# A selective state-space layer on one Trainium2 core: C rows by DMA broadcast, four of sixteen C products on GpSimd, three states in the ring

## What is computed

```
xn = layernorm(x);  x_inner, z = split(xn @ W_in.T)          # 256 features each
u = silu(depthwise conv of x_inner, 4 taps, causal)
dt_low, B, C = split(u @ W_x.T, [64, 80])                    # B and C: 16 numbers a token
dt = clip(softplus(dt_low @ W_dt.T + b_dt) + 0.001, 0.001, 0.1)
per token:  h = exp(dt * A) * h + (dt * u) * B               # h: 256 features x 16 states
            y = sum over the 16 states of h * C
y = (y + u * D_param) * silu(z);   x = x + y @ W_out.T
```

## Time and profile before

| | us |
|---|---|
| median of 3 runs | 4296.08 |
| the profiled execution | 4291.76 |
| its span | 4289.7 |
| VectorE busy in the span | 2998.2 (70%) |
| TensorE busy | 3517.0 (82%) |
| GpSimd busy | 1574.8 (37%) |
| ScalarE busy | 1881.7 (44%) |

### The profile page before, as it was taken

The page is one execution under the profiler, slowest core; times in us unless marked ns, Lnnn a source line. Parts: engine busy times, 40 slices in busy tenths (PEclk is TensorE's granted clock), DMA queues, the critical chain, the costliest instruction groups (busy, mean ns, idle before and its releaser), DMA issues. The chain is left out here.

```text
span 4289.7 us, 60121 instructions
## 1 busy us (share of the span) xinstructions
PE 3517.0 (82%) x21245; PEld 2138.2 (50%) x21300; DVE 2998.2 (70%) x6467; ACT 1881.7 (44%) x3383; POOL 1574.8 (37%) x1050
## 2 busy tenths in 40 slices
PE   5899999878999972777558888888859999999757
PEld 3666665556777762444323333333326666666423
DVE  7888887556777746333259999999975666666695
ACT  2555555325666630222146666666632223222224
POOL 2211110442111100688747877787741000011132
PEclk9999999989999975899879999999989999999868
DMA  6333332004444440233322222222220000000001
GB/s 145 85 80 79 79 79 59 1 13 108 98 98 98 99 131 9 40 44 43 71 69 67 79 69 66 64 79 68 66 71 1 1 1 1 1 1 1 10 0 40
DMA packets 196474, 237.43 MB, mean 55 GB/s; under 512 B 37554, under 2 KB 148883, under 8 KB 185924
## 3 DMA queue, kind: packets, MB, share of 16 engines
q1 hardware_dynamic: 170516, 214.93, 19.0%
q0 software_dynamic: 22528, 17.32, 2.9%
q10 hardware_dynamic: 3136, 1.35, 0.1%
HBM read 176.83 MB, written 55.51 MB: 54 GB/s over the span
## 5 line engine op out<-in xcount | busy, mean ns | idle before, releaser
L568 DVE TENSOR_REDUCE a_Mx<-a_Sx 128x2 f32<-128x512 f32 (+1 forms) x1024 | 590.8, 617 | 232.4 <-PE a_Sx L620 135.3
L2141 POOL TENSOR_TENSOR a_inp<-a_dtu,a_Bs 128x1024 f32<-128x1024 f32 x256 | 604.7, 2383 | 94.7 <-DVE a_h L2305 93.4
L2305 DVE TENSOR_TENSOR_SCAN a_h<-a_dA,a_inp 128x1024 f32<-128x1024 f32 x256 | 584.3, 2282 | 5.3 <-ACT a_dA L2233 5.3
L2395 PE MATMUL a_Y<-a_hc,g_ident 128*128 128x512 f32 x1024 | 520.0, 633 | 8.1 <-DVE a_hc L2315 8.0
L413 ACT ACTIVATE a_Pr<-a_Se 128x512 f32<-128x512 f32 x512 | 305.1, 596 | 410.9 <-DVE a_Se L562 219.4
L344 POOL TENSOR_TENSOR a_rest<-a_qk,a_parts 128x512 f32<-128x512 f32 x64 | 75.2, 1175 | 987.5 <-ACT a_parts L396 987.5
L2233 ACT ACTIVATE a_dA<-a_dtA,a_A 128x512 f32<-128x512 f32 x512 | 331.4, 682 | 171.8 <-DVE a_h L2305 171.1
L1957 ACT ACTIVATE f_sg<-f_GB 128x512 f32<-128x512 f32 x272 | 162.4, 597 | 513.5 <-PE f_GB L2007 513.4
L617 PE MATMUL a_Sx<-att_Kp,att_Qp 96*128 96x256 bf16 (+1 forms) x2048 | 347.4, 262 | 48.9 <-DMA att_Qp<-a_crows 26.0
L1902 DVE TENSOR_TENSOR f_sg<-f_sg,f_UB 128x512 f32<-128x512 f32 x256 | 176.2, 688 | 283.1 <-PE f_CB L2014 256.1
L2040 PEld LDWEIGHTS f_OUT<-f_wd,f_hm 128*128 128x128 f32 x2176 | 286.2, 192 | 91.0 <-issue 81.9
(11 more groups left out here) (446 smaller groups left out, 7136.2 us busy)
## 6 DMA issues: line engine op xcount, KB each, us to landing
a_Bs<-a_brows SPq DMA_DIRECT2D x256, 256.0 KB, 3.2
att_Qp<-a_packing SPq DMA_DIRECT2D x192, 192.0 KB
att_Kp<-a_packing SPq DMA_DIRECT2D x192, 192.0 KB
a_packing<-a_parts SPq DMA_DIRECT2D x64, 384.0 KB
a_packing<-a_parts SPq DMA_DIRECT2D x64, 128.0 KB
g_x<-x SPq DMA_DIRECT2D x8, 512.0 KB, 7.3
f_sum<-g_x SPq DMA_DIRECT2D x1, 4096.0 KB, 13.2
f_w<-L_w SPq DMA_DIRECT2D x2, 2048.0 KB
```

The lines of the kernel that those rows point to most:

```text
L568: nc.vector.tensor_reduce(Mx[(k + 2 - (j < LATE)) % 2][:, t, 2 * jj:2 * jj + 2], Sx[t][:, 0:2 * wd].rearrange("p (h q) -> p h q", h=2), AX ...
L2141: nc.gpsimd.tensor_tensor(inp[n % Q][:], dtu[k][:], Bs[n % Q][:].unsqueeze(1).to_broadcast([P, CH, GT]), ALU.mult).then_inc(s["mulB"], 1)
L2305: nc.vector.tensor_tensor_scan(h[n % 2][:].rearrange("p c q -> p (c q)"), dA[m % 2][:].rearrange("p c q -> p (c q)"), inp[n % Q][:].rearra ...
L2395: nc.tensor.matmul(Y[c][:], ident[:], hc[n % Q][:, c], start=(n == 0), stop=(n == N - 1))\
```

## The change

- C rows now come like B rows: `brows` holds 32 rows, and SP issues a second DMA for each state, into `Cs[n % 4]` in SBUF. `spread_C`, `split`, the matrix `sel` and its load go away, as does the bf16 copy on ScalarE (L2204).
- The C product reads h and Cs. For n = 1, 4, 7 and 10 (`MOVED`) GpSimd does it, after its `mulB` of n + 3; for the other twelve VectorE does it.
- `h` has three buffers; the scan of m waits for the product of m - 3.
- The skip term is a float32 matmul with a diagonal matrix, two a group, that opens Y's sum. VectorE's step at n = 0 becomes yy = Y * sz (two products of 512), and GpSimd's product with sz goes away.
- The add to x and its statistics (n = 15) move behind VectorE's C product of n = 15.

```diff
-        h = [sc.sb(f"h{i}", [P, CH, GT]) for i in range(2)]
+        h = [sc.sb(f"h{i}", [P, CH, GT]) for i in range(HR)]
+        Q, HR = 4, 3
+        MOVED = (1, 4, 7, 10)
+        Cs = [sc.sb(f"Cs{i}", [P, GT]) for i in range(Q)]
+        diag = sc.sb("diag", [P, CH, P])
-        CC = sc.ps("CC", [P, GT])
-                 (bdt, "bdt"), (dpar, "dpar"), (lnw, "lnw"), (lnb, "lnb"), (la, "la"), (sel, "sel")]
+                 (bdt, "bdt"), (dpar, "dpar"), (lnw, "lnw"), (lnb, "lnb"), (la, "la")]
@@ block.sync @@
+                    if on(0):
+                        wait_product(sp, g * N + n - Q)
+                        sp.dma_start(Cs[n % Q][:], bass.AP(brows.tensor, (k * 2 * N + N + n) * GT, [[0, P], [1, GT]]))\
+                            .then_inc(c_in[n % Q], 16)
@@ block.gpsimd @@
+            def mulC(m, n):
+                wait(pool, c_in[n % Q], 16 * (m // Q + 1))
+                wait(pool, s["scanned"], m + 1)
+                wait(pool, s["y_mm"], CH * (m + 1 - Q))
+                C = Cs[n % Q][:].unsqueeze(1).to_broadcast([P, CH, GT])
+                nc.gpsimd.tensor_tensor(hc[n % Q][:], h[m % HR][:], C, ALU.mult).then_inc(s["mulC_pool"], 1)
-                    if on(-1) and n == 1:
-                        wait(pool, s["y_read"], g * CH)
-                        wait(pool, s["sz_ready"], g)
-                        wait(pool, s["out_mm"], g - 1)
-                        nc.gpsimd.tensor_tensor(yy[:], yy[:], sz[(k + 1) % 2][:], ALU.mult).then_inc(s["y_ready"], 1)
-                    if on(1) and n == 9:
-                        split(g + 1, (k + 1) % 2)
+                    if n - 1 in MOVED and on(0):
+                        mulC(g * N + n - 1, n - 1)
@@ block.vector @@
-                        nc.vector.scalar_tensor_tensor(out=yy[:, c], in0=u[k][:, c], scalar=dpar[:, c:c + 1],
-                                                       in1=Y[c][:], op0=ALU.mult, op1=ALU.add).then_inc(s["y_read"], 1)
+                        nc.vector.tensor_tensor(yy[:, c], Y[c][:], sz[k][:, c], ALU.mult).then_inc(s["y_read"], 1)
-                        wait(v, s["mulC"], m - 1)
+                        wait_product(v, m - HR)
-                    if on(0):
-                        wait(v, s["cc_mm"], m + 1)
+                    if on(0) and n not in MOVED:
+                        wait(v, c_in[n % Q], 16 * (m // Q + 1))
                         wait(v, s["scanned"], m + 1)
                         wait(v, s["y_mm"], CH * (m + 1 - Q))
-                        nc.vector.tensor_tensor(hc[n % Q][:], h[n % 2][:], CC[:].unsqueeze(1).to_broadcast([P, CH, GT]),
+                        nc.vector.tensor_tensor(hc[n % Q][:], h[m % HR][:], Cs[n % Q][:].unsqueeze(1).to_broadcast([P, CH, GT]),
                                                 ALU.mult).then_inc(s["mulC"], 1)
@@ block.tensor @@
-                    if on(0) and n < N - 1:
-                        spread_C(g * N + (n + 1), n + 1, k)
                             wait(pe, s["y_read"], CH * g)
+                            for c in range(CH):
+                                nc.tensor.matmul(Y[c][:], diag[:, c], u[k][:, c], start=True, stop=False)
-                        wait(pe, s["mulC"], g * N + n + 1)
+                        wait_product(pe, g * N + n)
```

More of the change, by code:

```diff
@@ L2098, in state_space, with by_vector, by_pool, wait_product @@
         loads = [(win, "win"), (cw, "cw"), (wdl, "wdl"), (wbc, "wbc"), (wdt, "wdt"), (wout, "wout"), (cbias, "cbias"),
-                 (bdt, "bdt"), (dpar, "dpar"), (lnw, "lnw"), (lnb, "lnb"), (la, "la"), (sel, "sel")]
+                 (bdt, "bdt"), (dpar, "dpar"), (lnw, "lnw"), (lnb, "lnb"), (la, "la")]
         U = 9
         b_in = [sc.sem(f"b_in{i}") for i in range(Q)]
+        c_in = [sc.sem(f"c_in{i}") for i in range(Q)]
+        def by_vector(m):
+            return m // N * (N - len(MOVED)) + sum(n not in MOVED for n in range(m % N + 1))
+        def by_pool(m):
+            return m // N * len(MOVED) + sum(n in MOVED for n in range(m % N + 1))
+        def wait_product(eng, m):
+            if m >= 0 and m % N in MOVED:
+                wait(eng, s["mulC_pool"], by_pool(m))
+            elif m >= 0:
+                wait(eng, s["mulC"], by_vector(m))
         @block.sync
@@ L2124, in _ @@
         def _(pool):
[L2125 to L2135, removed]
             def mulB(m, n, k):
@@ L2366, in front @@
                         .then_inc(s["f_mm"], 1)
-            def spread_C(m, n, k):
-                wait(pe, s["mulC"], m)
-                nc.tensor.matmul(CC[:], sel[:, N + n], bc[k][:], start=True, stop=True).then_inc(s["cc_mm"], 1)
             def step(g, k, on):
                 for n in range(N):
-                    if on(0) and n < N - 1:
-                        spread_C(g * N + (n + 1), n + 1, k)
-                    if on(1) and n == N - 1:
-                        wait(pe, s["bc_ready"], 2 * g + 4)
-                        spread_C(g * N + N, 0, (k + 1) % 2)
                     if on(1):
@@ L2392, in step @@
                             wait(pe, s["y_read"], CH * g)
-                        wait(pe, s["mulC"], g * N + n + 1)
+                            for c in range(CH):
+                                nc.tensor.matmul(Y[c][:], diag[:, c], u[k][:, c], start=True, stop=False)
+                        wait_product(pe, g * N + n)
                         for c in range(CH):
-                            nc.tensor.matmul(Y[c][:], ident[:], hc[n % Q][:, c], start=(n == 0), stop=(n == N - 1))\
+                            nc.tensor.matmul(Y[c][:], ident[:], hc[n % Q][:, c], start=False, stop=(n == N - 1))\
                                 .then_inc(s["y_mm"], 1)
             straight(pe, step, GROUPS, 1, back=1)
[L2401 to L2405, removed]
 def program(nc, a, out):
@@ L2457, in l2_attn @@
     w = {n: a["L2_" + n] for n in "win cw wdl wbc wdt wout cbias bdt dpar lnw lnb la".split()}
-    state_space(nc, res, "a4", {**w, "sel": a["c_bsel"]})
+    state_space(nc, res, "a4", w)
 def l2_ffn(nc, res, a):
@@ L2537, in layout @@
     o["L2f_bias"] = np.broadcast_to(i["L2_ffn_e_score_bias"].reshape(1, 1, 32), (P, G, 32))
-    for n, c in {**attention_constants(), **choose_constants(), **routed_constants(), **state_constants()}.items():
+    for n, c in {**attention_constants(), **choose_constants(), **routed_constants()}.items():
         o["c_" + n] = c
```

32 lines of the change are left out of this document (15 added, 17 removed).

## The result

The changed kernel takes 4461.12 us (median of 4 runs, 4460.09 to 4463.38), 1.0384 times the time before (95% interval 1.0371 to 1.0397), or +165.5 us against 4295.59, the median of the four runs of the kernel before that were timed with it. The forecast was 4384, range 4315 to 4450. The direction and the main mechanism were right; a second stall, of 88 us, was missed, and the time lies above the range.

What follows compares the result with a forecast made beforehand. VectorE was taken to set the pace. 16 x 2.6 for the states plus 15 x 3.45 at group edges minus 6 gives +87 us on 4291.8, and with 4.3 for the median 4384 us; range 4315 to 4450.

Steps and rivals of the forecast that it cites:

- The exclusion: VectorE products with two SBUF inputs and GpSimd products take turns at a lock held for a whole instruction; 79%.
- three states: In states 1 to 10, each cycle of three takes 11.4 us instead of 10.5; +2.6 us a group.
- the stretch from scan 10 to the next scan 1: The group's edge, 28.8 us before the change; claimed to grow by 2.4 to 4.5 us a group.
- The near tie: After scan 15, GpSimd and VectorE reach the lock 0.1 us apart; unsettled, so the middle, 3.45 us a group, was taken.
- the forecast's upper case: GpSimd goes first after scan 15: scan 1' ends at 33.3 us, +4.5 us a group.
- SP asks for C row n once product n-4 is done ... hidden: SP's extra C loads come over 10 us ahead of use; cost nothing, at worst 51 us.
- The sign that the forecast gave for being wrong: A Cs load named as releaser of VectorE; listed among signs that would show the forecast wrong.
- The range: 4315, a little under the lock-never-idle floor, to 4450, the roof plus a late C row each group (51 us).
- the 6 us off for start and tail: No `sel` load at the start, no GpSimd product in the tail, no first split and copy: 6 us off.
- moved add now covers that: At the group's edge, the moved add covers VectorE's yy being held up by Y at the lower clock.
- Rival 1: No exclusion in this layer: groups of 54.4 us, -6.0 a group, 4194 us; 9%.
- Rival 2: GpSimd wins the lock after scans and TensorE falls to 1.2 GHz: +6.6 us a group, 4490 us; 9%.
- Rival 3: Half an exclusion: instructions shut each other out for part of their time; 4289 us, no change; 3%.

Runs made afterwards that it cites:

- e3: The changed kernel with SP's store behind the loads of n = 11 and VectorE's twelve C products reading ones in PSUM (C left out there): 4220.86 us, ratio 0.9853.
- e1: The changed kernel with SP's store of the next B and C rows, and its wait, moved behind the loads of n = 11: 4375.4 us, ratio 1.0209.
- e7: The kernel before with only the skip term on TensorE, yy * sz on VectorE and the moved add; C as it was: 4277.17 us, ratio 0.9987.
- e4: e1 with MOVED empty, so VectorE does all sixteen C products from SBUF: 4346.51 us, ratio 1.0148.
- e8: e6 with GpSimd's split moved from n = 9 to n = 12: 4247.52 us, ratio 0.9885.
- e5: e1 with ScalarE copying each C row that VectorE needs from SBUF to a PSUM tile: 4302.21 us, ratio 1.0041.
- e6: e1 with VectorE's twelve states getting C in PSUM by the earlier split and spread matmuls, GpSimd's four rows by DMA: 4353.13 us, ratio 1.0162.

## Why the prediction was right and wrong

- **The exclusion** was right: that it would hold here, argued from the first layer's rows, is shown by e3. Its working held: three states 11.36 us for 11.4, products at 1.28 and 3.31 for 1.3 and 3.2 (its own timeline gives 3.3 for the second, from 5.88 to 9.19), the stretch from scan 10 to the next scan 1 33.16 us in e1 (2706.06 to 2739.22):

```profile
2706.06 4.46 DVE L2314 TENSOR_TENSOR_SCAN a_h<-a_dA,a_inp 128x1024 f32<-128x1024 f32 x2
...
2728.09 3.30 DVE L2324 TENSOR_TENSOR a_hc<-a_h,a_Cs 128x1024 f32<-128x1024 f32 x1
...
2736.30 3.00 DVE L2324 TENSOR_TENSOR a_hc<-a_h,a_Cs 128x1024 f32<-128x1024 f32 x1
2739.22 4.46 DVE L2314 TENSOR_TENSOR_SCAN a_h<-a_dA,a_inp 128x1024 f32<-128x1024 f32 x2
```

- **The near tie** at scan 15 goes to GpSimd in every group but the last, both in the changed kernel and in e1 (the product of n = 15 takes 3.3 us): 33.2 us, the forecast's upper case of 33.3, and not the middle. 15 x 0.9 = 14 us too little.
- **"SP asks for C row n once product n-4 is done ... hidden"** is the step that failed. The wait named there was the right one for the load itself, but the load is in a queue, and ahead of it, in the same step of the program, stood another wait: for the next group's bf. I counted the loads that came to SP's queue and not what they were put behind. The term stood at nothing in the sum and was bounded at 51 us, by the 3.2 us of one landing a group; it is 6.0 us a group, since the issue itself came late: 88.1 us of idle, 75 of them net. The sign that the forecast gave for being wrong, a Cs load named as what VectorE waits for, is what came. The trace of the kernel before could have shown it. There the C product of state 9 starts at 2789.43, and SP comes past that wait only at 2790.59:

```profile
2789.43 1.22 DVE L2315 TENSOR_TENSOR a_hc<-a_h,a_CC 128x1024 f32<-128x1024 f32 x1
```

```profile
2790.59 0.32 SPq L2112 DMA_DIRECT2D a_brows<-a_bf  x1
2790.95 7.24 SPq L2118 DMA_DIRECT2D a_Bs<-a_brows  x5
```

  A load behind it lands at 2790.95 + 3.2 = 2794.15 at the earliest, 4.7 us after that product's place (an estimate from these rows): about 71 us in fifteen groups, before a line was changed.
- **The range** took its upper end from that bound. With the tie and the stall as measured the sum is 87 + 14 + 75 = 176 against 165.5. Two more terms were off, and they pull against each other. The group of the kernel before was put at 60.4 us from one group; its fifteen stretches from `dtA` to `dtA` are 60.8 on the mean (911.9 us), and those of e1 67.1 (1006.8) where the upper case has 67.5. So fifteen groups cost 95 us more in e1, where the sum with the tie as measured has 15 x (2.6 + 3.45 + 0.9) = 104. And the 6 us off for start and tail did not come: from the layer's first reciprocal (L90) to the first `dtA` it took 47.6 us before, 48.6 in the changed kernel and 47.3 in e1, the tail 77.2, 79.1 and 79.1. The first and the last `dtA`, before, in the changed kernel and in e1:

```profile
L2277 DVE TENSOR_SCALAR a_dtA<-a_et x16: 685/686/694, 2200.8 to 3112.7; 128x1024 f32<-128x1024 f32 x16
```

```profile
L2286 DVE TENSOR_SCALAR a_dtA<-a_et x16: 684/686/693, 2199.2 to 3281.3; 128x1024 f32<-128x1024 f32 x16
```

```profile
L2286 DVE TENSOR_SCALAR a_dtA<-a_et x16: 684/686/694, 2187.4 to 3194.2; 128x1024 f32<-128x1024 f32 x16
```

  The changed kernel's 1082.1 us are 170 more than before and 75 more than e1.
- **That e1 by its ratio (4385) meets the forecast (4384) is partly luck.** The tie was 14 us too cheap, the fifteen groups were otherwise 9 too dear, and start and tail, with the last group's 2.6, were 5 too cheap (-3.4 for +1.6 in e1's trace): 97 us between the two traces. That the ratio has 90 is left open. The forecast's own sum, 4291.8 + 87 + 4.3, gives 4383.
- **"The moved add now covers that"**, of the wait for Y, was right (2.9 us of idle at yy are left of 18.7), but e7 shows that in the kernel before most of the gain was taken back elsewhere. It was not a term of its own in the sum.
- **Rival 1** had the right sign for a kernel without the exclusion: 4194 by its sum, 4233 by e3's ratio. Its nine states were 1.2 us a group too short (29.4 us from scan 1 at 2716.13 to scan 10 at 2745.51, with one late decay in them, for 28.2) and the rest of the group 2.0 (28.2 for 26.2).
- **Rival 2** did not come: in e4's inner states, with a full ring, VectorE's product goes first; and though the clock in the window fell from 0.97 to 0.91, VectorE waits for Y for 2.9 us in all. **Rival 3** did not either: a product that finds GpSimd at work waits for the whole rest of its instruction (3.31).
- The Trainium skill's rule ("SBUF — State Buffer", SBUF: two separate sides) agrees with every run here: two SBUF operands of a product collide, one does not. The 115 ns that its section on the bandwidth-pool intuition gives, measured there on a DMA whose descriptors GpSimd has to write, are not seen on top of the holds taken from the rows: after the product that ends at 2741.83 (2738.53 + 3.30 in the changed kernel) the waiting mulB ends at 2744.04, 2.21 later, as in the earlier trace rows, and three states come to 11.36 for 11.4. Whether a part of those 2.21 us is a handover, no run here can tell.

## What to carry to other kernels

Before work goes to GpSimd, look at which of VectorE's instructions beside it read two SBUF tiles: in this layer they take turns with it (and so does `et`, with one SBUF operand), and the waiting is booked as busy time, so that a mean duration which has grown is the sign. With one operand in PSUM the same four products on GpSimd made the kernel faster (e3, e8), but only where nothing else came late: e5 and e6, with one operand in PSUM too, were slower than the kernel before. And a DMA that joins a queue inherits every wait ahead of it in program order: give it the lead of its neighbours, or put the waits of other stages behind it (here 75 us for moving three lines). The trace of the kernel before shows when the queue gets past such a wait.

## What the runs showed that I had not expected

- Moving work off the busiest engine to an idle one made the kernel slower by 26 us (e1 against e4); without the exclusion the like move made it faster by 44 (e8 against e7).
- The order at the lock has a pattern: VectorE first if both wait for the same scan (1.23 us for the product in e4's inner states), GpSimd first if it comes straight from its last product (3.30). Both are margins of about 0.1 us, an estimate from the starts in the earlier trace rows and the pitch in the earlier trace rows.
- A copy of 0.6 us on an engine that is busy 72% of the time cost VectorE 113.5 us of waits (e5), and a split of 4.6 us on GpSimd cost 119 us more at one place than at another (e6, e8).
